# Weight transposes of the q, k and v stage moved from a seam between blocks into the matmul stream of the block ahead

## What is computed

```
xn = layernorm(x)                                   # x: 8 x 2048 x 2048
q, k, v = xn @ Wq.T + bq, xn @ Wk.T + bk, xn @ Wv.T + bv
phi_q, phi_k = elu(q) + 1, elu(k) + 1
context = phi_q * cumsum(phi_k * v, over tokens) * SCALE
s = context @ Wo.T + bo
z = fwht(xn * SU_ug)                                # Hadamard transform
h = silu(z @ W_gate.T * c1) * (z @ W_up.T * c2)     # 8192 wide
g = silu(fwht(h * SU_dp) @ W_down.T * c3)
out = x + s * g
```

## Time and profile before

| what | us |
|---|---|
| median of 3 runs | 4985.62 |
| lowest and highest run | 4796.01 and 5174.11 |
| the profiled execution, time | 4798.55 |
| the profiled execution, span of its slowest core (core 5) | 4796.6 |
| stage B on core 5, first transpose to the end of its last product | 133.6 to 922.4 |

### The profile page before, as it was taken

The page is one execution under the profiler, slowest core; times in us unless marked ns, Lnnn a source line. Parts: engine busy times, 40 slices in busy tenths (PEclk is TensorE's granted clock), DMA queues, the critical chain, the costliest instruction groups (busy, mean ns, idle before and its releaser), DMA issues. The chain is left out here.

```text
span 4796.6 us, 64833 instructions; the slowest of 8 cores (4773.0 to 4796.6 us)
## 1 busy us (share of the span) xinstructions
PE 4085.2 (85%) x26502; PEld 2413.8 (50%) x26502; DVE 930.3 (19%) x1434; ACT 1240.4 (26%) x1889; POOL 224.5 (5%) x422
## 2 busy tenths in 40 slices
PE   2899999679419999999999999999669996699952
PEld 2444444344104444444444444444458885588841
DVE  6344545312690111011111011111000000000003
ACT  3333333210112222222222222222640004600002
POOL 0000000011000000000000000000000000000000
PEclk9999999879659999999999999999999998899975
DMA  4321211231002222222222222221642324522248
GB/s 143 58 53 36 53 36 40 67 84 56 14 9 57 53 52 50 53 53 53 53 53 53 53 53 53 53 53 36 114 110 81 89 72 88 130 80 81 81 135 291
DMA packets 215502, 340.02 MB, mean 71 GB/s; under 512 B 12256, under 2 KB 168112, under 8 KB 207024
## 3 DMA queue, kind: packets, MB, share of 16 engines
q0 software_dynamic: 39456, 167.80, 17.7%
q1 hardware_dynamic: 175760, 168.09, 11.4%
HBM read 394.58 MB, written 75.50 MB: 98 GB/s over the span
## 5 line engine op out<-in xcount | busy, mean ns | idle before, releaser
L905 PE MATMUL ps_dn<-yslab,wdTp 128*128 128x256 bf16 x8192 | 898.5, 273 | 40.5 <-DMA yslab<-y 40.5
L689 PE MATMUL ps_up<-z,wupT 128*128 128x512 bf16 x4096 | 928.0, 380 | 1.2 <-ACT wgT L734 1.2
L695 PE MATMUL ps_g<-z,wgT 128*128 128x512 bf16 x4096 | 925.8, 379 | 0.0
L905 PEld LDWEIGHTS ps_dn<-yslab,wdTp 128*128 128x128 bf16 x8192 | 803.4, 98 | 135.5 <-issue 40.9
L695 PEld LDWEIGHTS ps_g<-z,wgT 128*128 128x128 bf16 x4096 | 400.8, 98 | 483.3
L689 PEld LDWEIGHTS ps_up<-z,wupT 128*128 128x128 bf16 x4096 | 396.0, 98 | 456.5 <-issue 4.5
L744 ACT ACTIVATE sg_t<-ps_g,gsc 128x512 f32<-128x512 f32 x256 | 175.9, 687 | 1412.5 <-PE ps_g L695 1412.5
L766 DVE SCALAR_TENSOR_TENSOR u_t<-ps_up,usc,sg_t 128x512 bf16<-128x512 f32 x256 | 192.3, 751 | 1763.5 <-ACT sg_t L744 1763.5
L919 ACT ACTIVATE gst<-ps_dn,dsc 128x256 bf16<-128x256 f32 x128 | 60.6, 473 | 818.5 <-PE ps_dn L905 818.5
L978 DVE TENSOR_TENSOR rT<-ssl,gsl 128x8192 bf16<-128x8192 bf16 x4 | 17.7, 4422 | 1265.3 <-DMA gsl<-gd 1265.3
L367 PE MATMUL ps_q<-xnT,wT 128*128 128x512 bf16 x1024 | 238.6, 387 | 23.5 <-ACT wT L379 23.5
(11 more groups left out here) (95 smaller groups left out, 2650.9 us busy)
## 6 DMA issues: line engine op xcount, KB each, us to landing
yslab<-y SPq DMA_DIRECT2D x128, 512.0 KB, 7.2
xt<-x SPq DMA_DIRECT2D x32, 1024.0 KB, 6.9
wupn<-wup POOLq DMA_DIRECT2D x64, 512.0 KB, 5.1
wgn<-wg POOLq DMA_DIRECT2D x64, 512.0 KB, 7.1
y<-ystage SPq DMA_DIRECT2D x64, 512.0 KB, 3.1
wdn<-wd POOLq DMA_DIRECT2D x16, 2048.0 KB, 15.1
out<-onat POOLq DMA_DIRECT2D x16, 1024.0 KB, 11.1
wnat<-wq POOLq DMA_DIRECT2D x16, 512.0 KB, 7.7
```

Source lines behind the costliest of these rows:

```text
L689: ins = e.matmul(ps_up[c % 2][:], wupT[j % 2][:, d * 128:(d + 1) * 128], z3[:, d, c * TC:(c + 1) * TC], start=(d == 0), stop=(d == NDT - 1))
L695: ins = e.matmul(ps_g[c % 2][:], wgT[j % 2][:, d * 128:(d + 1) * 128], z3[:, d, c * TC:(c + 1) * TC], start=(d == 0), stop=(d == NDT - 1))
L905: ins = e.matmul(ps_dn[et % 4][:], wdTp3[:, et, a2, :], yslab3[ts % 2][:, a2, :], start=(a2 == 0), stop=(a2 == 63))
```

## The change

TensorE's loop over the fills and ScalarE's loop over the copies become functions of a block and a weight (`bfills` and `bevacs`). Both run for the first block ahead of the loop. Within the loop the fills for block a + 1 follow the chunks of block a: those of Wq behind chunk 0, those of Wk behind chunk 1, those of Wv behind chunk 2. ScalarE's copies follow `b_k` of the same chunk. The wait for the three loads goes with the fills of Wq, and the wait for all six copies stays at the head of each block's matmuls. Buffers, sizes, counts and the streams of VectorE, POOL and SP are as before.

```diff
                 @blk.tensor
+                    def bfills(aa, w):
+                        if w == 0:
+                            dwait(e, s_wsl, aa, 3)
+                        for f in range(2):
+                            fill = 6 * aa + w * 2 + f
+                            if fill >= 2:
+                                e.wait_ge(s_wtrE.h, fill - 1)
+                            for d in range(8):
+                                dt = f * 8 + d
+                                ins = e.transpose(ps_wtr[fill % 2][:, d * 128:(d + 1) * 128],
+                                                  wnat[w][aa % 2][:, dt * 128:(dt + 1) * 128], identb[:])
+                            s_wtrF.inc(ins)
+
+                    for w in range(3):
+                        bfills(0, w)
                     for a in range(NA):
-                        dwait(e, s_wsl, a, 3)
-                        gf = 6 * a
-                        for w in range(3):
-                            for f in range(2):
-                                fill = gf + w * 2 + f
-                                if fill >= 2:
-                                    e.wait_ge(s_wtrE.h, fill - 1)
-                                for d in range(8):
...
-                                s_wtrF.inc(ins)
                         e.wait_ge(s_wtrE.h, 6 * (a + 1))
                         for c in range(NTC):
...
                                 s_mm.inc(ins)
+                            if a + 1 < NA and c < 3:
+                                bfills(a + 1, c)
 
                 @blk.scalar
+                    def bevacs(aa, w):
+                        for f in range(2):
+                            fill = 6 * aa + w * 2 + f
+                            e.wait_ge(s_wtrF.h, fill + 1)
+                            s_wtrE.inc(e.copy(wT[w][aa % 2][:, f * 1024:(f + 1) * 1024], ps_wtr[fill % 2][:]))
+
+                    for w in range(3):
+                        bevacs(0, w)
                     for a in range(NA):
-                        for fill in range(6 * a, 6 * a + 6):
-                            w, f = divmod(fill - 6 * a, 2)
-                            e.wait_ge(s_wtrF.h, fill + 1)
-                            s_wtrE.inc(e.copy(wT[w][a % 2][:, f * 1024:(f + 1) * 1024], ps_wtr[fill % 2][:]))
                         for c in range(NTC):
...
                             s_bk.inc(e.activation(b_k[p][:], a_k[p][:], AF.Exp, bias=0.0, scale=-1.0))
+                            if a + 1 < NA and c < 3:
+                                bevacs(a + 1, c)
```

More of the change, by code:

```diff
@@ L339, in _ @@
                     if not on("B"): return
-                    for a in range(NA):
-                        dwait(e, s_wsl, a, 3)
-                        gf = 6 * a
-                        for w in range(3):
-                            for f in range(2):
-                                fill = gf + w * 2 + f
-                                if fill >= 2:
-                                    e.wait_ge(s_wtrE.h, fill - 1)
-                                for d in range(8):
-                                    dt = f * 8 + d
-                                    ins = e.transpose(ps_wtr[fill % 2][:, d * 128:(d + 1) * 128],
-                                                      wnat[w][a % 2][:, dt * 128:(dt + 1) * 128], identb[:])
-                                s_wtrF.inc(ins)
+                    def bfills(aa, w):
[12 more added lines that the diff above has]
+                        bfills(0, w)
+                    for a in range(NA):
                         e.wait_ge(s_wtrE.h, 6 * (a + 1))
```

## The result

| | before | changed |
|---|---|---|
| median of 6 runs, us | 4890.82 | 4729.68 |
| lowest run, us | 4793.75 | 4727.07 |
| profiled execution, time, us | 4798.55 | 4730.32 |
| span of its slowest core, us | 4796.6 (core 5) | 4728.5 (core 1) |

The ratio of the changed kernel's time to that of before is 0.9863, with a 95% interval from 0.9845 to 0.988: 1.4% faster. Some executions had cores at a lower granted clock; only the medians of the table include them, all ratios and single times leave them out, and rows are taken from cores without it.

What follows compares the result with a forecast made beforehand. Stage B was taken as bound by TensorE except at its seams, there by ScalarE's copies out of PSUM. Seams 60.0 us and clock 5.1 us, together 65 us, took 4798.55 us to 4733 us; range 4716 to 4762 us.

Steps and rivals of the forecast that it cites:

- The seam term: At 15 seams between blocks of stage B: 6.70 - 3 x 0.90 = 4.00 us saved each, 60.0 us.
- The clock term: First q groups of stage B: three falls of the granted clock vanish with the waits, 3 x 1.69 = 5.1 us.
- The covers: Stage B: ScalarE's copies, VectorE's scan and product, and POOL's loads (lead 65 us) stay hidden, cost 0.
- The first (waits at the insertions): Each of 45 insertions in stage B keeps a 0.80 us wait: gain only 29 us, 4769 us; chance 0.06.
- The second (clock falls behind each insertion): Matmul groups behind stage B's insertions: 45 x 1.69 = 76 us lost against 60 gained, 4815 us; chance 0.03.
- The third (late load): Chunk 0's insertion stalls when a weight landing exceeds the 65 us lead: about 4800 us and up; chance 0.01.
- A measurement of this kernel can tell about 2% from no change: Whole kernel's time: 2% is 96 us, while the forecast sum is 1.4%.
- within 2%: Whole kernel's time changes by no more than 2% either way; chance 0.94, with 0.03 each for faster and slower.

Runs made afterwards that it cites:

- e1: Changed kernel with all 48 transposes of the next block and their six copies behind chunk 0; core spans up to 4754.0 us, stage B 758.5 us against 721.1.
- e2: Changed kernel with the insertions behind chunks 1, 2 and 3 instead of 0, 1 and 2; 4756.4 us.
- e6: Changed kernel with VectorE running each block's scan twice, one behind the other; 4731.6 us.
- e7: Changed kernel with POOL's weight load also waiting for the value group of chunk 2 two blocks before the load's; 4727.2 us.
- e3: Changed kernel with every fill of an insertion written six times, 96 transposes each; 4928.2 us.
- e4: Changed kernel with TensorE waiting for VectorE's product pv at the head of blocks 1 to 15, no transposes there; its total time is not in the text.
- e10: Changed kernel, first two blocks' weight loads after stage A's tile 8, six row tiles of Wo loaded in stage B; ratio to before 0.9799.
- e9: Changed kernel with the weight loads of blocks 0 and 1 issued at the start of stage A instead of stage B; ratio to before 0.9874.

## Why the prediction was right, and where not

**The seam term: right.** The insertion was taken as 0.90 us from stage E and is 0.89 to 0.90 us; a period went from 48.13 to 44.12 us. 15 x 4.0 = 60 us. e1 and e2 show each half: with more than two fills at a time the waits between them return, and without a free chunk behind the last the wait for the last copy does.

**The clock term: right in its mechanism, and a little small.** Forecast 3 x 1.69 = 5.1 us. All falls inside the stage are gone; the q groups went from 238.6 to 231.5 us, 7.1 us. The other 2 us are block 0's first group, whose part at the lower level differs from core to core and execution to execution (core 3 of the same execution has 234.3 us). They are luck and not an effect of the change. Together 60.2 + 0.3 (two seams that were a little longer) + 5.1 + 2.1 = 67.7 us, which is stage B's difference. I forecast 65 us and 4733 us; the profiled execution took 4730.3, 68.2 us less.

**The covers: right.** ScalarE, VectorE and POOL's loads cost nothing, as argued. e6 shows that the scan could be twice as long, and e7 that the load could have 43 us less.

**The rivals.** The first (waits at the insertions) did not come: 3.4 us of waits on copies are left, all of block 0. The second (clock falls behind each insertion) did not come, and e3 rules its cause out: not the transposes but the pauses let the clock fall, as e4 shows without any transposes. Its price was also put too high: the 4798.55 us already hold the three falls of before, 5.1 us, so 45 falls would have given 4810 us and not 4815, and 39 falls, not 36, would have used up the gain. In the wording of the Trainium skill ("TensorE: Matmul & The Clock Gate", Part 4) transposes do not count as busy for the clock gate in the same way; e3's granted clock of 1.00 over 5.4 us runs of them disagrees, and so does the rise from 0.50 to 0.99 under transposes alone in e10; the measurement decides. The third (late load) has its threshold between 10 and 21 us of lead, not at 65.

**What failed.** One step: "A measurement of this kernel can tell about 2% from no change". The prediction had no row for these 2%, and with them it forecast a time that could not be told from no change. The interval of the measured ratio is 0.9845 to 0.988, under 0.2% to each side, so the gain of 1.4% is more than seven times what the measurement leaves open. The 0.94 on "within 2%" holds as a number, but that nothing measurable would come is wrong: the sum of 65 us was the forecast of a clear gain. The prediction's own numbers spoke against the 2%: the profiled execution stood 0.05% above the lowest run. The lowest three of before lie between 4793.75 and 4796.01 us, and five of the changed kernel's six between 4727.07 and 4730.65 us.

What stays open: which seams see a fall. A 2.02 us pause alone gives 11 of 15, a 1.93 us pause behind 16 transposes 1 to 6 of 15, before's seam with 3.21 us in five pauses 2 or 3 of 15, and e1's 1.75 us in four pauses none. The longest single pause seems to count more than the sum, but no run varied it alone. The pauses do not decide by themselves either. On cores 0, 2, 5 and 6 of before the falls stand 242.4 us apart, which is five blocks, though the waits at the seams between are alike; in e4 core 1 has six falls in a row, then three seams without one, then five in a row, all behind the same 2.02 us. So it also matters at what moment a pause comes, and what sets that moment was not tested.

## What to carry to other kernels

Where an engine stops at a seam for a relay over another engine (transpose, copy, matmul), put no more of it in one place than there are buffers, and leave a piece of stream behind the last of it that is longer than the relay's latency: here three insertions of 0.90 us, 2.70 us together, instead of 6.70 us for a seam. If a later stage of the same kernel is already built that way, look there for the price: stage E's 0.90 us was the insertion's price here to 0.01 us. And a short pause of TensorE can cost more than itself: in e4 2.02 us of idle time cost (52.7 - 1.5) / 15 = 3.4 us on average, block 0's 1.5 us left out.

## What the runs showed of the hardware that I had not expected

- A pause of TensorE of 2.02 us between dense groups is followed by a stretch at the lower clock level at 11 of 15 seams on each of four cores (granted clock 0.67 over the next group, 5.30 instead of 3.61 us).
- 96 transposes in a row, 5.36 us, keep the granted clock at 1.00, 45 times in a stage (e3), and transposes with short waits took it from 0.50 to 0.99 in e10's stage C.
- With six weight tiles in flight stage C got one every 3.8 us, against 4.6 us with two; and in e9 6 MB of weights read beside the token tiles made stage A 8.6 us (core 2) and 12.7 us (core 0) longer, half and nine tenths of the 17.6 and 14.0 us of waiting that they took away.
